# Routing in small pieces over seven rounds, and another order of the prologue, in a kernel of attention and routed experts

## The reference

```python
xn = _layernorm(x, axis=-1)                     # x: 4 x 512 x 256, no gain or bias
s = _L0_attn_ref(xn, Wq, Wk, Wv, Wo)            # 16 heads of 128, 4 key/value heads
g = _silu(_L0_ffn_ref(xn, gate_w, w_gate_up, w_down, shared_gate_up, shared_down))
x = x + s * g
# attention: rope and xpos scale on q and k, causal softmax(q k / sqrt(128)) v, then Wo
# experts, on the 2048 tokens of 256:
logits = jnp.einsum('th,eh->te', x, gate_w)     # 16 experts
scores = jax.nn.softmax(logits, axis=-1)
topk_w, topk_idx = jax.lax.top_k(scores, 2)
# y = sum over the two experts chosen, weighted, of swiglu(x @ w_gate_up[e]) @ w_down[e]
#     (inner size 176), plus swiglu(x @ shared_gate_up) @ shared_down (inner size 352)
```

## Time and profile before

| | |
|---|---|
| median of 3 runs | 742.27 us (741.11 to 743.2) |
| the profiled execution | 736.88 us, span of its instructions 735.0 us |
| busy in the span | PE 657.2 us (89%), DVE 579.7 (79%), POOL 535.8 (73%), PEld 457.5 (62%), ACT 441.6 (60%) |
| chain that ended last, over the span | POOL 27%, PE 27%, DVE 21%, issue 16%, ACT 7% |
| granted TensorE clock, mean | 0.982 |

### The profile page before, as it was taken

One profiled execution on the slowest core, in us unless ns is written; L12 is line 12 of the kernel. 1 busy time (PEld: TensorE's weight loads), 2 busy tenths in 40 slices (PEclk: granted clock), 3 DMA queues, 4 the chain that ended last, 5 costly groups with the idle time before them and its releaser, 6 DMA issues.

```text
span 735.0 us, 16494 instructions
## 1 busy us (share of the span) xinstructions
PE 657.2 (89%) x4995; PEld 457.5 (62%) x4996; DVE 579.7 (79%) x1682; ACT 441.6 (60%) x1206; POOL 535.8 (73%) x584
## 2 busy tenths in 40 slices
PE   2678889999898899999999999999998999999992
PEld 1244667666565666666666666666666777777760
DVE  7988797999989798898888898889886454333378
ACT  3575755576555566665666566666767764555542
POOL 4577766688756788988989898898898973555510
PEclk9999999999999999999999999999999999999996
DMA  9582000005000000000000000000042634565772
GB/s 302 169 264 84 1 1 3 1 1 148 2 1 1 1 15 16 15 14 14 21 15 22 14 14 14 14 14 15 17 62 82 188 86 107 138 141 138 215 280 100
DMA packets 65104, 50.61 MB, mean 69 GB/s; under 512 B 35392, under 2 KB 58400, under 8 KB 65056
## 3 DMA queue, kind: packets, MB, share of 16 engines
q1 hardware_dynamic: 60944, 39.45, 19.3%
q0 software_dynamic: 3840, 10.52, 4.4%
q10 hardware_dynamic: 272, 0.02, 0.0%
HBM read 24.73 MB, written 18.96 MB: 59 GB/s over the span
## 4 chain that ended last, share of the span: by engine, by line
POOL 27%; PE 27%; DVE 21%; issue 16%; ACT 7%; DMA 1%; POOLq 0%; DVEq 0%; ACTq 0%
POOL arena L558 12%; PE bank L1553 9%; POOL arena L545 6%; PE bank L1583 6%; ACT arena L777 4%; POOL arena L552 3%; POOL xs_dram L591 3%; DVE arena L1109 3%; DVE arena L1084 3%; DVE arena L1083 3%; PE bank L1396 2%; POOL compare L587 2%; PE bank L1562 2%; PE bank L1409 2%; PE bank L1441 2%
## 5 line engine op out<-in xcount | busy, mean ns | idle before, releaser
L558 POOL TENSOR_TENSOR arena<-arena,rinv 128x128 f32<-128x128 f32 (+3 forms) x256 | 176.4, 720 | 78.6 <-DVE rinv L1103 78.6
L777 ACT ACTIVATE arena<-bank,nmax 128x512 f32<-128x512 f32 (+3 forms) x256 | 132.5, 534 | 66.0 <-DVE nmax L1097 66.0
L1097 DVE CUSTOM_DVE_ANT_0 bank<-bank,mask_b 128x512 f32<-128x512 f32 (+3 forms) x256 | 118.1, 516 | 12.7 <-issue 12.6
L1396 PE MATMUL bank<-arena 128*128 128x512 f16 (+7 forms) x768 | 117.9, 304 | 5.9 <-POOL arena L552 5.7
L785 ACT CAST arena<-bank 128x512 f16<-128x512 f32 (+1 forms) x192 | 93.4, 523 | 45.3 <-PE bank L1409 44.9
L1365 PE MATMUL bank<-xnT_hi,arena 128*128 128x512 f16 (+1 forms) x320 | 110.2, 386 | 9.7 <-DVE arena L1084 7.2
L1425 PE MATMUL bank<-arena 128*128 128x512 f16 (+7 forms) x768 | 114.8, 299 | 0.0
L1409 PE MATMUL bank<-ident_f,arena 128*128 128x128 f32 x640 | 93.4, 277 | 21.9 <-POOL arena L558 12.0
L1109 DVE TENSOR_TENSOR arena<-bank,arena 128x512 bf16<-128x512 f32 (+1 forms) x192 | 108.8, 594 | 4.9 <-ACT arena L785 3.7
L545 POOL TENSOR_TENSOR arena<-arena 128x512 f32<-128x512 f32 x77 | 98.8, 1283 | 5.0 <-DVE arena L1084 3.9
L1441 PE MATMUL bank<-arena 128*128 (+2 forms) x768 | 95.2, 275 | 3.0 <-DVE logit L1051 2.4
(11 more groups left out here) (145 smaller groups left out, 1164.0 us busy)
## 6 DMA issues: line engine op xcount, KB each, us to landing
xs_dram<-s_sb SPq DMA_DIRECT2D x4, 1548.0 KB, 14.9
stage<-w_gate_up SPq DMA_DIRECT2D x16, 352.0 KB
arena<-ys_dram SPq DMA_DIRECT2D x8, 512.0 KB, 6.6
stage<-w_down SPq DMA_DIRECT2D x16, 176.0 KB
stage<-wq SPq DMA_DIRECT2D x4, 512.0 KB, 8.7
stage<-wo SPq DMA_DIRECT2D x4, 512.0 KB, 6.3
stage<-x SPq DMA_DIRECT2D x1, 2048.0 KB, 11.0
out<-s_sb SPq DMA_DIRECT2D x8, 256.0 KB, 2.1
```

What stands on the lines that cost most here:

```text
L558: ins = pool.tensor_tensor(pr, pr, rinv[:, par, qt:qt + 1].to_broadcast([P, (qt + 1) * P]), ALU.mult)
L777: ins = act.activation(probs[par][:, P_AT[qt]:P_AT[qt] + n], score_bank[u][:, col:col + n], ACT.Exp, scale=-1.0, bias=nmax[:, par, qt:qt + ...
L1097: ins = dve.tensor_tensor_reduce(score_bank[u][:, col:col + n], score_bank[u][:, col:col + n], mask_b[:, S - n:S], -1.0, 3e38, ALU.add, AL ...
L1396: ins = pe.matmul(score_bank[u][:, col:col + n_k], qT[a][:, j * S + qt * P:j * S + (qt + 1) * P], kT[m][:, 0:n_k], start=(n == 0), stop=(n ...
```

## The change

*The prologue.* The key is projected and roped first, then q0. GpSimd waits for the first normalisation before its first two low halves of weights, and the third and fourth are computed later, both on GpSimd (the fourth was VectorE's, L1141). VectorE takes the statistics of batches 2 and 3 and the variances of batches 1 to 3 behind the maxima of head 0 instead of ahead of the ropes. ScalarE takes their square root behind the exponentials of head 0 and the copy of q2.

*The x items* all come in round 0, one or two at the end of each head; so do both of the later normalisations.

*The routing.* The router is cut into four parts, one at the end of each head of round 1. Maxima, indices and all later steps are cut into pieces that VectorE takes in `routing(rd, at)`: at 0 ahead of the rope of q0, at 1 and 2 ahead of the low half of a head's output, at 3 ahead of the last maxima. They reach from round 1 into round 6. Two operations of the ranks go to GpSimd (`rank_sums`). The ranks' matmuls move to the first head of round 4, the groups of tiles to the end of round 6.

*GpSimd's extra work* (low halves of weights, routing, row splits, scatters) all moves into `ahead_of_division(rd, j)`, between the rope's sum and the division. The scatter of a round's first tile is issued in two halves, ahead of the divisions of j = 1 and j = 2; that of the second with both halves ahead of the last division. Rounds 6 to 13 remain the scatter rounds, of which 7 to 13 are the loop.

```diff
-ITEMS_PROLOGUE = ["q0", "k", "q1", "q2", "q3"]
-ITEMS_FIRST = ["q0", "v", "x10", "q1", "x11", "x20", "k", "x21", "q2", "q3"]
-ITEMS_SECOND = ["q0", "v", "q1", "o0", "x30", "k", "o1", "x31", "q2", "o2", "q3", "o3", "logit"]
-ITEMS_RANK = ["q0", "v", "q1", "o0", "k", "o1", "rank", "q2", "o2", "q3", "o3"]
-ITEMS_TILE = ["q0", "v", "q1", "o0", "k", "o1", "tile", "q2", "o2", "q3", "o3"]
+ITEMS_PROLOGUE = ["k", "q0", "q1", "q2", "q3"]
+ITEMS_FIRST = ["q0", "v", "x10", "q1", "x11", "x20", "k", "x21", "x30", "q2", "q3", "x31"]
+ITEMS_LOGITS = ["q0", "v", "g0", "q1", "o0", "g1", "k", "o1", "g2", "q2", "o2", "q3", "o3", "g3"]
+ITEMS_RANK = ["q0", "v", "rank", "q1", "o0", "k", "o1", "q2", "o2", "q3", "o3"]
+ITEMS_TILE = ["q0", "v", "q1", "o0", "k", "o1", "q2", "o2", "q3", "o3", "tile"]
...
-X_BEFORE = [[], ["x10"], ["x20"]]
-X_AFTER = [[], ["x11"], ["x21"]]
-X_SECOND = [[], ["x30"], ["x31"]]
-LOOP_FROM, LATE = 6, NG - 2
-assert 2 * (LATE - LOOP_FROM) == NT
+X_AT = [["x10"], ["x11", "x20"], ["x21", "x30"], ["x31"]]
+
+
+SCATTER_FROM, LOOP_FROM, LATE = 6, 7, NG - 2
+assert 2 * (LATE - SCATTER_FROM) == NT
 
...
-EARLY_ITEMS = [ITEMS_FIRST, ITEMS_SECOND, ITEMS_LOOP, ITEMS_LOOP, ITEMS_RANK, ITEMS_TILE]
-WEIGHTS_AT = {(0, 0): 4, (0, 1): 5, (1, 0): 6, (1, 1): 7, (2, 0): 8, (3, 1): 9}
-WEIGHTS_BY = [4, 6, 8, 9, 10, 10]
-ROUTE_AT = {(2, 0): 0, (2, 2): 1, (3, 2): 2, (4, 1): 3}
+EARLY_ITEMS = [ITEMS_FIRST, ITEMS_LOGITS, ITEMS_LOOP, ITEMS_LOOP, ITEMS_RANK, ITEMS_LOOP, ITEMS_TILE]
+WEIGHTS_AT = {(0, 1): 4, (0, 3): 5, (1, 1): 6, (1, 3): 7, (2, 1): 8, (3, 3): 9}
+WEIGHTS_HI_AT = {(0, 0): 4, (0, 2): 5, (1, 0): 6, (1, 2): 7, (2, 0): 8, (3, 1): 9}
+WEIGHTS_BY = [4, 6, 8, 9, 10, 10, 10]
...
-            for n in range(W_FIRST - 1):
+            pool.wait_ge(xn_first, QT)
+            for n in range(W_URGENT):
                 weights_lo(n)
...
+            rotate_lo("k", PROLOGUE.rot("k"))
             rotate_lo("q0", PROLOGUE.rot("q0"))
-            rotate_lo("k", PROLOGUE.rot("k"))
             rotate_sum("q1", PROLOGUE.item("q1"))
+            weights_lo(2)
             rotate_lo("q1", PROLOGUE.rot("q1"))
+            weights_lo(3)
             divide(0, 0)
             rotate_lo("q2", PROLOGUE.rot("q2"), ROT_BUF_PROLOGUE)
...
-            def scatter():
-                for n in range(TOP_K):
+            def scatter(halves=range(TOP_K)):
+                for n in halves:
...
+            def rank_sums():
+                pool.wait_ge(scanned, 1)
+                pool.tensor_tensor(count, total[:], count, ALU.subtract).then_inc(offset_ready, 1)
+                pool.wait_ge(offset_ready, 1)
+                pool.tensor_tensor(slot[:], slot[:], count.rearrange("p e t -> p t e"), ALU.add).then_inc(offset_ready, 1)
...
+            def ahead_of_division(rd, j):
+                if j == 1 and rd.late:
+                    shared_lo(0)
+                if j == 3 and rd.late:
+                    shared_lo(1)
+                if rd.pair and j in (1, 3):
+                    t = rd.tiles()[j // 2]
+                    pool.wait_ge(rows_ready, t + 1)
+                    rows_low(t)
+                    pool.wait_ge(rows_split, t + 1)
+                    pool.sem_inc(rows_written, 1)
+                    scatter((0,) if j == 1 else (0, 1))
+                if rd.pair and j == 2:
+                    scatter((1,))
+                if (rd.early, j) in WEIGHTS_AT:
+                    weights_lo(WEIGHTS_AT[rd.early, j])
+                if rd.early == 2 and j == 3:
+                    shift_logits()
+                if rd.early == 3 and j == 1:
+                    choose()
+                if rd.early == 3 and j == 3:
+                    select()
+                if rd.early == 4 and j == 1:
+                    weigh()
+                if rd.early == 4 and j == 3:
+                    rank_sums()
+                if rd.early == 5 and j == 1:
+                    tag()
+                if rd.early == 5 and j == 3:
+                    slots()
+
...
-                    if j == 1 and rd.late:
-                        shared_lo(0)
-                    if j == 1 and tiles_:
-                        pool.wait_ge(rows_ready, tiles_[0] + 1)
-                        rows_low(tiles_[0])
+                    ahead_of_division(rd, j)
                     divide(rd.head(j + 1), (j + 1) % 2)
...
-                    if j == 1 and tiles_:
-                        pool.wait_ge(rows_split, tiles_[0] + 1)
-                    if j == 1 and tiles_:
-                        scatter()
-                    if rd.early == 3 and j == 0:
-                        choose()
-                    if (rd.early, j) in WEIGHTS_AT:
-                        weights_lo(WEIGHTS_AT[rd.early, j])
                     if rd.last:
                         expert_lo(j)
-                    if rd.early == 2 and j == 1:
-                        shift_logits()
-                    if rd.early == 4 and j == 0:
-                        weigh()
-                    if rd.early == 5 and j == 0:
-                        tag(rd)
-                    if rd.early == 5 and j == 2:
-                        slots()
...
+                    if rd.first and j == 2:
+                        pool.wait_ge(fill_out, 16 * FILLS)
+                        pool.memset(fill[:, :, D + 1], 0.0).then_inc(zeroed, 1)
...
-                    if rd.late:
-                        shared_lo(1)
-                    if rd.pair:
-                        pool.wait_ge(rows_ready, tiles_[1] + 1)
-                        rows_low(tiles_[1])
+                    ahead_of_division(rd, GH - 1)
                     divide(rd.head(GH), 0)
-                    if rd.pair:
-                        pool.wait_ge(rows_split, tiles_[1] + 1)
                     rotate_lo("q2", rd.rot("q2"))
-                    if rd.pair:
-                        scatter()
-                    if rd.first:
-                        pool.wait_ge(fill_out, 16 * FILLS)
-                        pool.memset(fill[:, :, D + 1], 0.0).then_inc(zeroed, 1)
-                    if rd.early == 3:
-                        select()
...
-            root_of(1)
...
-            rotate_hi("q0", PROLOGUE.rot("q0"))
+            rotate_hi("k", PROLOGUE.rot("k"))
...
-            rotate_hi("k", PROLOGUE.rot("k"))
+            rotate_hi("q0", PROLOGUE.rot("q0"))
             exponentials(0, 0, (0,))
             rotate_hi("q1", PROLOGUE.rot("q1"))
             exponentials(0, 0, (1, 2))
+            rotate_hi("q2", PROLOGUE.rot("q2"), ROT_BUF_PROLOGUE)
+            root_of(1)
             normalise(1)
-            rotate_hi("q2", PROLOGUE.rot("q2"), ROT_BUF_PROLOGUE)
...
-                        if rd.first:
-                            x_items_hi(rd, X_BEFORE[j])
                     if rd.first:
-                        x_items_hi(rd, X_AFTER[j])
-                    if rd.early == 1:
-                        x_items_hi(rd, X_SECOND[j])
-                    if rd.early in (0, 1) and j == 0:
-                        normalise(2 + rd.i)
-                    if (rd.early, j) in WEIGHTS_AT:
-                        weights_hi(WEIGHTS_AT[rd.early, j])
+                        x_items_hi(rd, X_AT[j])
+                    if rd.first and j < 2:
+                        normalise(2 + j)
+                    if (rd.early, j) in WEIGHTS_HI_AT:
+                        weights_hi(WEIGHTS_HI_AT[rd.early, j])
...
-            statistics(1)
             for c in range(KC):
                 xnT_lo_part(0, c, xnT_bank[c][:]).then_inc(xnT_lo, 1)
-            statistics(2)
-            variances(1)
...
+            def ranks_out(rd):
+                rank_bank = misc_bank[rd.bank("rank")]
+                dve.wait_ge(misc_ps, rd.item("rank"))
+                dve.wait_ge(indexed, QT)
+                dve.tensor_copy(count, rank_bank[:, NT * E_ROUTED:2 * NT * E_ROUTED].rearrange("p (t e) -> p e t", e=E_ROUTED)).then_inc(copied, 1)
+                dve.tensor_copy(slot[:], rank_bank[:, 0:NT * E_ROUTED].rearrange("p (t e) -> p t e", e=E_ROUTED)).then_inc(misc_free, 1)
+
+            def scan_counts():
+                dve.wait_ge(copied, 1)
+                flat = count.rearrange("p e t -> p (e t)")
+                dve.tensor_tensor_scan(total[:].rearrange("p e t -> p (e t)"), flat, flat, 0.0, ALU.add, ALU.max).then_inc(scanned, 1)
+
...
-            for name in ("q0", "k"):
+            for name in ("k", "q0"):
                 first_rope(name)
                 first_sum(name)
             first_rope("q1")
-            hi, lo = w_split(W_FIRST - 1)
-            dve.wait_ge(w_hi, W_FIRST)
-            dve.wait_ge(w_lo, W_FIRST - 1)
-            dve.tensor_tensor(lo, w_stage(W_FIRST - 1), hi, ALU.subtract).then_inc(w_lo, 1)
             dve.wait_ge(const_cast, 4)
             dve.wait_ge(mask_zero, 1)
             row_max(0, 0)
+            statistics(2)
+            first_rope("q2", PROLOGUE.rot("k"), (0, 0))
+            first_sum("q2")
+            variances(1)
             invert_roots(1)
```

(64 more changed lines are left out.)

169 lines of the change are left out of this document (87 added, 82 removed).

## The result

The changed kernel took 723.71 us (median of 4 runs, 722.32 to 725.1) beside 741.69 for the kernel before on the same chip (4 runs, 740.73 to 743.2): a ratio of 0.975, with a 95% interval of 0.9728 to 0.9773. That is 18.0 us faster, two thirds of the 26.8 us forecast. Both kernels were run again later on another chip, with a profile each; there they took 718.47 and 736.69, 18.2 us apart.

The account below looks back on a forecast made before the run. VectorE was taken to pace plain rounds, with stalls in early rounds and GpSimd late but not full in scatter rounds; terms summed to -26.8 us, 736.9 to 710.1, plus 5.4 to the runs' median: 715.5, range 707 to 730.

Parts of the forecast that it names:

- rival (a): Scatter rounds: GpSimd remains the bound and waits move to other divisions; 32.2 us a round, 724.5 in all; chance 0.18.
- rival (b): Early rounds keep their stalls and round 1's clock still falls; half of rounds 0, 1, 4, 5; 723; chance 0.16.
- The plain round: A round without routing or scatters: 30.1 us, VectorE setting the pace with 1.3 us to spare.
- Rounds 2 to 5: Routing pieces spread over plain rounds of 30.1 us: -1.0, +0.5, -2.4 and -4.6 us for the four rounds.
- The scatter rounds: Row splits and issues fill GpSimd's waits ahead of divisions: 30.9 us a round, 1.6 gained, -11.2 over 7 rounds.
- Round 0: x items move to each head's end; two x items and a normalisation come in from round 1: -2.0 us.
- Round 6: Scatters as before, gets 2.4 us of VectorE work from round 5, gains 1.9 from GpSimd's order: +0.5 us.
- Round 1: Router in four parts; its stall and lower clock go; 33.4 us, a change of -6.2.
- The prologue: Head 0's maxima 5.4 us earlier, mostly used up by late statistics, variances and table loads: -0.4 at round 0's mark.
- Rival (d): Slower: ScalarE's copies wait for a scatter's later half and delay the heads' output copy, in 8 rounds; chance 0.04.
- a sign of being wrong: Listed signs: scatter rounds still at 32 us, ScalarE waiting for a scatter, or a first mark after 46.

Follow-up runs that it names:

- experiment 6: Changed kernel with late statistics and variances ahead of the ropes, ScalarE's root before the first exponentials, inversion behind head 0's maxima: 716.98 us, ratio 0.9748.
- best_x3: Changed kernel with row split before rope's sum, round 6 comparison earlier, prologue rearranged, x30, x31 and last normalisation back in round 1: 708.48 us, ratio 0.963.
- experiment 2: Changed kernel with the scatter rounds' order on GpSimd as before the change, scatters behind the low half that follows the division: 723.24 us, ratio 0.9805.

## Why the forecast was right in sign and too large

Its sum was -26.8; measured were -18.0 by the medians and -19.6 by the second pair of profiles. The 7.2 us between are made of errors of both signs. The time itself, 723.7, lies nearer to the prices of rival (a), 724.5, and rival (b), 723, than to the 715.5 forecast; that is a coincidence in part, since each of the two happened only in some of its rounds, as the stages show.

**The plain round** was the step that failed under most others: "without it the round is 31.27 - 1.19 = 30.1 us ... VectorE sets the pace there". One engine's busy time plus its waits isn't a bound when two others are nearly as full. The runs showed a cluster: TensorE busy for 30.6 to 31.1 in every one of these rounds, and 0.2 to 0.4 us back for some 0.9 us of VectorE's operations. By that, the plain round is about 30.9 (estimate: 31.27 less a quarter to two fifths of 1.19). The same error made me count routing pieces in full on top of 30.1. They cost less than their durations: round 2 holds 1.0 us more of VectorE's work than round 3 (30.82 and 29.78) and takes 0.35 us longer. Rounds 2 to 5 came in 0.7 to 1.5 us under the forecast (31.4, 31.1, 32.3, 31.4 for 32.4, 31.8, 33.8, 32.9), 4.6 us together.

**The scatter rounds** gave 0.8 a round and not 1.6, 5.8 us short in all and the largest part of the miss. The placing does what it says: the 2.7 us of waiting before divisions fell to 0.7, and putting the scatters back takes all 5.4 us of the gain away. What I had missed is the 0.82 us between the end of the row split and the scatter that waits for it, twice a round; "0.2 for each issue's gap" was the only gap that I priced, and the earlier trace rows couldn't show this one, since the division covered it. I took each move's cost as its own duration, and not the wait that lost its cover. Removing it gives 0.5 a round (3.8 us in rounds 6 to 13), and the other engines' work takes the rest. Rival (a) was half right: the chain stayed all GpSimd, at 31.7, between my 30.9 and its 32.2.

**Round 0** was the largest miss of a single round, -2.0 against +2.4. "8.6 becomes some 7.3 twice, and 0.6 is added at the end" counted VectorE's and TensorE's halves of the three things that came in, and not where ScalarE does its normalisation: between exponentials and the copy that VectorE waits for. Without the three, and with a clock of 1.00, round 0 takes 34.12 us, close to the 34.7 forecast for it with them. Nor had I counted that the changed prologue leaves TensorE idle for 5.45 us, and the round begins at the lower clock; no run prices that alone.

**Round 6**, +0.5 against +2.0: the scatters' new order placed a comparison of 128x16 beside three consecutive GpSimd operations, 3.40 us instead of 0.22 to 0.74. The mechanism was in my prediction, in the prologue, where I priced what VectorE loses beside GpSimd; I didn't ask which of the moved pieces it would hit next.

**Round 1** was right in mechanism and nearly in size (34.31 for 33.4): the router's stall is gone and the clock granted there is 1.00, where it was 0.73. **The prologue** came out at -0.5 and +0.4 for -0.4: the early maxima (4.9 us for 5.4), the statistics in their way and the loads all appeared as forecast. That the late statistics and the second root together cost 2 us is shown by experiment 6, which moves both. What I had not seen is the third weight's landing, on which the first mark now hangs; between 44.42 and 45.77 it moves by more than the term itself, so that the number came true is partly luck.

**Rival (b)** is refuted for rounds 1 to 5 and true of round 0. **Rival (d)'s** mechanism is there: ScalarE waits 0.6 us a round for the landing of a scatter, which I had named as a sign of being wrong and priced at nothing. It is on no chain that I looked at; no run removed it alone, so its price stays open, at most 0.6 a round. That round 14 gained 0.5 us was not forecast. It hangs on the scatters' place in the rounds before it, since experiment 2, which changes only that, takes it back; by what way is open.

## What to carry to other kernels

Before moving an instruction, ask what its old neighbour was hiding: a wait for one's own result costs nothing behind a 2.7 us division and 0.82 us when it stands bare. Put short VectorE operations that read SBUF where GpSimd is known to wait, for instance ahead of the operation that GpSimd waits for. And when three engines are each over 90% busy in a round, a microsecond saved on one is worth a fraction of it (here 0.3 us for 1.0 of TensorE or 0.9 of VectorE, nothing for 2.5 of GpSimd): take the floor from the rounds that already run best, not from one engine's busy time.

## What the hardware showed that I had not expected

- A 128x16 operation of VectorE was held for 3.2 us beyond its 0.22 by three back-to-back GpSimd operations of 2.74, 1.15 and 1.25 us; so were two operations of 12 columns, for 0.9 and 1.9 us. GpSimd's own operations beside them were not longer than elsewhere (1.15 and 2.13 us).
- From the end of GpSimd's row split to the start of the DMA issue that waits for it GpSimd stood idle for 0.82 us (0.98 once, in the second profile); an issue without such a wait followed after 0.16.
- A table load on ScalarE cost 1.28 us and, at two places with work right ahead of it and behind it, no more than 0.02 us on either side.
- TensorE's granted clock fell to its lower level at 39.3 in the changed kernel, 4.3 us into a stretch of 5.45 us in which TensorE had no work, and stayed there for 10.2 us; in "best_x3" it was at the upper level from 35.2 on, through rounds 0 and 1.
